# Projections as pairs of 64-column matmuls, and transposes as float32 matmuls with the identity, in a pipelined attention and ternary layer

## The chip, the cores and the metric

The kernel runs on one core of one Trainium2 chip. The metric is device time in microseconds (us). Of the kernel before, three runs took 470.35, 467.87 and 469.35 us; the median is 469.35.

## What is computed

The input x holds 32 sequences of 256 tokens with 128 features, in float32. Cut to what matters:

```python
def _L0_attn_ref(x, W_qkv, b_qkv, W_out, b_out):
    qkv = x @ W_qkv + b_qkv                    # 16 query heads, 4 key/value heads, 8 wide
    q, k, v = jnp.split(qkv, [DIM, DIM + KV_DIM], axis=-1)
    ...
    scores = jnp.einsum('bkgsd,bktd->bkgst', q, k) / np.sqrt(HEAD_DIM)
    scores = jnp.where(causal, scores, -jnp.inf)
    attn = jax.nn.softmax(scores, axis=-1)
    y = jnp.einsum('bkgst,bktd->bkgsd', attn, v)
    ...
    return y @ W_out + b_out

def _L0_ffn_ref(input, weight, alpha, bias):
    delta = 0.7 * jnp.mean(jnp.abs(weight))
    w = jnp.where(weight > delta, 1.0, jnp.where(weight < -delta, -1.0, 0.0)) * alpha
    return jnp.einsum('bsd,od->bso', input, w) + bias

x = x + _layernorm(_L0_attn_ref(_layernorm(x), ...))
x = x + _layernorm(_L0_ffn_ref(_layernorm(x), ...))
```

## The kernel before

All of x stays on chip in one tile X. The work on the 32 sequences is a pipeline written out by hand: in step t each engine runs its part of a fixed list once, and each function works on sequence t minus a lag of its own. The lags are NORM 0, PROJ 1, SPLIT 2, MAX 3, TURN 4, ATT 5, DIV 6, OUT 7, MID 8, FFN 9, and the store comes last, so there are 42 steps. There is no loop on the device and no scheduler: the order in which each engine meets its work is the order of the calls in its own `step`, and semaphores between engines do the rest. Each engine works strictly in that order, so a wait holds back all that stands behind it.

TensorE's `step` (L939 to L968) mixes short groups of matmuls. Scores (`st`, L813) and the products for the row maxima (`mx`, L862) are bf16 matmuls that fill 64 columns of the array each; they come in pairs, one for output partitions 0 to 63 and one for 64 to 127. The value projection (`v`, L877) does the same in float32. Attention times values (`pv`, L834) uses four 32-column matmuls, float32. Between them stand the groups that the change touches, all with 128 columns: `op` (L890, output projection, from tile yn), `x1` (L910, transposes of the normed input xn1), `ff` (L918, the ternary layer), `qk` (L927 and L928, query and key projection) and `x3` (L936, transposes of xn3). `turn` (L900) transposes the 16-row maxima. Two transposes of 128x128 are in `x1` and two in `x3`. All these groups, and `v`, write one shared PSUM bank, `ps_w`; `take` (L789) makes each wait until the user before it in ORDER = v, op, turn, x1, ff, qk, x3 has been read out.

The readers, with their places in their engines' orders:
- ScalarE: `take_y` (L477, copy of ps_y), exp 0 (L455), `second_part` (L491, bf16 split), exp 1, `take_turned` (L498), exp 2, `take_xn1` (L506), exp 3, exp 4, two norms of A (L468), `take_qk` (L513, L514), exp 5, `first_part` (L484), `take_xn3` (L522), two norms of F (L468).
- VectorE: two groups of row maxima (L651), `take_v` (L699), statistics (L609), `split_max` (L725 and L727: a cast of the maxima to bf16 and its remainder), moments (L621), `take_a` (L708, which frees ps_w from `op`), then more maxima, a reciprocal (L735), statistics, `take_f` (L716) and the norms (L628).
- GpSimd (POOL): `third` (L415, third part of the split), the inverse roots (L392 to L399), an addition (L407), `remainder` (L430), `divide` (L423, which writes yn), another addition (L407).
- SyncE (SP) issues every DMA of the steady steps in one queue; among them are the denominators (L328), their reciprocals to DRAM and back, spread over the partitions (rden, L343), and every fourth step a load and a store of 512 KB each.

In `pe.transpose` and `pe.matmul` alike the profile lists one or two TensorE records for each call: one for a transpose and for a bf16 matmul, two for a float32 matmul.

Of the kernel before, what the change touches and what calls it, by code (L numbers as in the profile page):

```python
# [11 lines left out]
B, S, D = 32, 256, 128  # L12
NH, NKV, HD = 16, 4, 8
G = NH // NKV
NLO = 2
# [17 lines left out]
NORM, PROJ, SPLIT, MAX, TURN, ATT, DIV, OUT, MID, FFN = range(10)  # L33
# [52 lines left out]
def build(nc, x, wq, wk, wv, wo, bq, bk, bo, wf, alpha, bf, ident, qfix, kfix, vmask, bvw, out):  # L86
    with ExitStack() as ctx:
        def sb(name, shape, dt):
            return ctx.enter_context(nc.sbuf_tensor(name, shape, dt))

        def psum(name, shape):
            return ctx.enter_context(nc.psum_tensor(name, shape, F32))

        def sem(name):
            return ctx.enter_context(nc.semaphore(name))


        wq_sb = sb("wq_sb", [D, 128], F32)
        wk_sb = sb("wk_sb", [D, 128], F32)
        wv_sb = sb("wv_sb", [D, 32], F32)  # L100
        wo_sb = sb("wo_sb", [128, NLO, D], F32)
# [7 lines left out]
        id_sb = sb("id_sb", [128, 128], F32)  # L109
# [12 lines left out]
        weff = sb("weff", [D, D], F32)  # L122
# [3 lines left out]
        xn1 = [sb(f"xn1_{i}", [128, TT, D], F32) for i in range(2)]  # L126
        xn1T = sb("xn1T", [128, S], F32)
# [20 lines left out]
        xn3 = [sb(f"xn3_{i}", [128, TT, D], F32) for i in range(2)]  # L148
        xn3T = sb("xn3T", [128, S], F32)
# [15 lines left out]
        ps_w = psum("ps_w", [128, 512])  # L165
# [22 lines left out]
        s_qk_ps = sem("s_qk_ps")  # L188
# [589 lines left out]
        def _(pe):  # L778
# [10 lines left out]
            def take(s, user):  # L789

                sm, v = last_work(s, user)
                if sm is not None:
                    pe.wait_ge(sm, v)
# [88 lines left out]
            def op(s):  # L882
                if s.on(OUT):
                    y = yn[s.b(OUT) % 2]

                    pe.wait_ge(s_yn, s.n(OUT, 1, 1))
                    take(s, "op")
                    for j in range(TT):
                        for lo in range(NLO):
                            last = pe.matmul(ps_w[:, D * j:D * j + D], y[:, lo, 128 * j:128 * j + 128],  # L890
                                             wo_sb[:, lo, :], start=(lo == 0), stop=(lo == NLO - 1))
                    last.then_inc(s_op_ps, 1)

            def turn(s):
# [9 lines left out]
            def x1(s):  # L904
                if s.on(PROJ):

                    pe.wait_ge(s_xn1, s.n(PROJ, 1, 1))
                    take(s, "x1")
                    for j in range(TT):
                        last = pe.transpose(ps_w[:, 128 * j:128 * j + 128], xn1[s.b(PROJ) % 2][:, j, :], id_sb[:])  # L910
                    last.then_inc(s_xt_ps, 1)

            def ff(s):
                if s.on(FFN):
                    pe.wait_ge(s_x3, s.n(FFN, 1, 1))
                    take(s, "ff")
                    for j in range(TT):
                        last = pe.matmul(ps_w[:, D * j:D * j + D], xn3T[:, 128 * j:128 * j + 128], weff[:],  # L918
                                         start=True, stop=True)
                    last.then_inc(s_ff_ps, 1)  # L920

            def qk(s):
                if s.on(PROJ):

                    pe.wait_ge(s_xt, s.n(PROJ, 1, 1))
                    take(s, "qk")
                    pe.matmul(ps_w[:, 0:S], wq_sb[:], xn1T[:], start=True, stop=True)  # L927
                    pe.matmul(ps_w[:, S:2 * S], wk_sb[:], xn1T[:], start=True, stop=True).then_inc(s_qk_ps, 1)  # L928

            def x3(s):  # L930
                if s.on(MID):

                    pe.wait_ge(s_xn3, s.n(MID, 1, 1))
                    take(s, "x3")
                    for j in range(TT):
                        last = pe.transpose(ps_w[:, 128 * j:128 * j + 128], xn3[s.b(MID) % 2][:, j, :], id_sb[:])  # L936
                    last.then_inc(s_x3_ps, 1)

            def step(s):  # L939
                st(s, 0)  # L940
                mx(s, 0)
                v(s)
                mx(s, 1)
                st(s, 1)
                mx(s, 2)
                op(s)
                st(s, 2)
                mx(s, 3)
                pv(s, 0)
                turn(s)  # L950
                st(s, 3)
                mx(s, 4)
                x1(s)
                pv(s, 1)
                pv(s, 2)
                ff(s)
                st(s, 4)
                mx(s, 5)
                qk(s)
                pv(s, 3)  # L960
                mx(s, 6)
                st(s, 5)
                mx(s, 7)
                pv(s, 4)
                x3(s)
                mx(s, 8)
                pv(s, 5)
                mx(s, 9)  # L968
# [63 lines left out]
```

## Time and profile before

| what | value |
|---|---|
| median of three runs | 469.35 us |
| the profiled execution | 467.76 us, span 465.9 us |
| TensorE matmuls (PE) | 413.6 us busy, 89% of the span, 6918 records |
| weight loads (PEld) | 287.2 us, 62% |
| VectorE (DVE) | 396.6 us, 85% |
| ScalarE (ACT) | 323.5 us, 69% |
| GpSimd (POOL) | 297.1 us, 64% |
| granted TensorE clock, mean | 0.965 of full |

Read it so: the busy share is over the whole span, with a filling stretch ahead of 89 us and an emptying one behind 404 us; in between, a step of the pipeline repeats. In a timeline each row is a group of like instructions in order of time: its start, how long from the first start to the last end, engine, line, operation, output and inputs, and the count. Matmuls overlap, so a group's end lies behind the start of the next; how long a group holds the engine is the distance from its start to the next group's start. The page's PEclk row shows 9 tenths or more of full speed in its 40 slices of 11.6 us, except for one slice at 8 (from 35 us) and the last three, at 7, 5 and 5 (from 431 us on).

### The profile page before, as it was taken

What the parts mean: (1) busy time and instruction counts of PE and PEld (TensorE: products, weight loads), DVE (VectorE), ACT (ScalarE), POOL (GpSimd) and SP (SyncE); (2) the same over time, 40 slices, a digit from 0 to 9 for tenths busy, and PEclk for the clock granted to TensorE, in tenths of its full rate; (3) what the DMA queues carried; (4) which work ended last, traced back from release to release, by engine and by line L of the source; (5) the groups of instructions that cost most, each with busy time, mean ns of one, the idle gap of its engine ahead of it and who ended that gap; (6) DMA issues with size and microseconds to landing.
All of it is one profiled execution on the core that took longest, in us unless ns stands there. A gap on an engine that the chain in (4) does not pass through costs nothing.

```text
span 465.9 us, 18300 instructions
## 1 busy us (share of the span) xinstructions
PE 413.6 (89%) x6918; PEld 287.2 (62%) x6918; DVE 396.6 (85%) x1307; ACT 323.5 (69%) x577; POOL 297.1 (64%) x552
## 2 busy tenths in 40 slices
PE   1478989999999999999999999999999999998541
PEld 1345657676776667676667677766777766664331
DVE  5768888999999899999999999989999998983441
ACT  1323877777787778788777777777888887767521
POOL 2523335567777677777777677767777776566663
PEclk9998999999999999999999999999999999999755
DMA  6454433354333633363334433363334333501211
GB/s 185 52 51 67 103 85 75 82 108 82 79 74 71 153 75 78 75 159 80 77 77 119 117 74 70 76 158 74 79 79 123 75 74 76 113 28 30 54 41 45
DMA packets 72255, 39.50 MB, mean 85 GB/s; under 512 B 13000, under 2 KB 68008, under 8 KB 72168
## 3 DMA queue, kind: packets, MB, share of 16 engines
q1 hardware_dynamic: 70832, 37.70, 36.8%
q8 instruction: 55, 0.90, 0.9%
q10 hardware_dynamic: 1336, 0.64, 0.5%
q14 instruction: 32, 0.26, 0.3%
HBM read 13.65 MB, written 4.72 MB: 39 GB/s over the span
## 4 chain that ended last, share of the span: by engine, by line
PE 58%; DVE 14%; DMA 8%; issue 7%; POOL 7%; ACT 2%; SPq 2%; ACTq 2%; POOLq 0%; DVEq 0%
PE ps_y L834 13%; PE ps_mx L862 11%; PE ps_st L813 11%; DVE M L651 7%; DMA den<-Y 5%; PE ps_w L890 5%; PE ps_w L927 4%; PE ps_w L918 4%; PE ps_w L928 3%; DVE stats L609 2%; POOL yn L423 2%; PE ps_w L936 2%; PE ps_w L910 2%; PE ps_w L900 2%; DVE Mp L725 1%
## 5 line engine op out<-in xcount | busy, mean ns | idle before, releaser
L651 DVE TENSOR_REDUCE M<-ps_mx 128x2 f32<-128x512 f32 (+3 forms) x448 | 218.6, 529 | 19.6 <-PE ps_mx L862 18.2
L455 ACT ACTIVATE PT<-ps_st 128x1024 f32<-128x1024 f32 (+1 forms) x192 | 168.6, 881 | 23.6 <-PE ps_st L813 12.5
L862 PE MATMUL ps_mx<-KS,QS 112*64 112x64 bf16 (+2 forms) x2560 | 130.6, 225 | 10.7 <-DMA KS<-part 6.4
L862 PEld LDWEIGHTS ps_mx<-KS,QS 112*64 112x64 bf16 x2560 | 88.2, 111 | 55.8 <-issue 26.6
L834 PE MATMUL ps_y<-PT,VB 128*32 128x256 f32 (+3 forms) x2048 | 103.0, 307 | 0.9 <-ACT PT L455 0.9
L813 PE MATMUL ps_st<-QS,KS 114*64 114x256 bf16 (+1 forms) x1024 | 103.7, 304 | 0.0
L395 POOL TENSOR_TENSOR rstd<-vareps,mhalf 128x2 f32<-128x2 f32 x128 | 88.8, 694 | 10.0
L430 POOL TENSOR_TENSOR rest<-QK,part 128x512 f32<-128x512 f32 x32 | 39.3, 1227 | 40.1 <-ACT part L484 40.1
L498 ACT CAST MpT<-ps_w 16x512 bf16<-16x512 f32 x32 | 18.4, 575 | 55.1 <-PE ps_w L900 55.1
L834 PEld LDWEIGHTS ps_y<-PT,VB 128*32 128x32 f32 x2048 | 40.3, 108 | 24.4 <-ACT PT L455 14.6
L813 PEld LDWEIGHTS ps_st<-QS,KS 114*64 114x64 bf16 x1024 | 47.1, 109 | 12.8 <-issue 2.2
L392 POOL TENSOR_TENSOR nmean<-mv,minus 128x2 f32<-128x2 f32 x64 | 12.6, 197 | 59.3 <-DVE mv L621 58.6
L423 POOL TENSOR_TENSOR yn<-Y,rden 128x512 f32<-128x512 f32 x32 | 40.9, 1277 | 9.2 <-DMA rden<-rec_dram 8.7
L890 PE MATMUL ps_w<-wo_sb,yn 128*128 128x128 f32 x256 | 38.4, 295 | 8.3 <-POOL yn L423 8.2
L393 POOL TENSOR_TENSOR vareps<-mv,eps 128x2 f32<-128x2 f32 x128 | 25.7, 201 | 30.8 <-DVE mv L621 30.8
L415 POOL TENSOR_TENSOR part<-rest,part 128x512 bf16<-128x512 f32 x32 | 37.2, 1163 | 6.1 <-ACT part L491 5.5
L628 DVE TENSOR_SCALAR xn<-X,mv,rstd 128x128 f32<-128x128 f32 x128 | 36.7, 344 | 5.1 <-POOL rstd L395 4.8
L890 PEld LDWEIGHTS ps_w<-wo_sb,yn 128*128 128x128 f32 x256 | 32.1, 197 | 11.3 <-POOL yn L423 10.1
L609 DVE BATCH_NORM_STATS2 stats<-X 128x6 f32<-128x128 f32 x128 | 29.0, 268 | 9.7 <-POOL X L407 7.2
L468 ACT ACTIVATE A<-A,shift,rstd 128x128 f32<-128x128 f32 x64 | 27.8, 483 | 12.1 <-POOL shift L399 12.0
L468 ACT ACTIVATE F<-F,shift,rstd 128x128 f32<-128x128 f32 x64 | 28.1, 487 | 3.3 <-POOL shift L399 3.3
L621 DVE BATCH_NORM_AGGREGATE mv<-stats 128x2 f32<-128x6 f32 x256 | 28.4, 160 | 1.9 <-issue 0.2
(62 smaller groups left out, 512.8 us busy)
## 6 DMA issues: line engine op xcount, KB each, us to landing
QS<-part SPq DMA_DIRECT2D x192, 64.0 KB
rden<-rec_dram SPq DMA_DIRECT2D x32, 256.0 KB
out<-X SPq DMA_DIRECT2D x8, 512.0 KB, 5.1
X<-in_x SPq DMA_DIRECT2D x7, 512.0 KB, 7.6
KS<-part SPq DMA_DIRECT2D x32, 96.0 KB
KS<-part SPq DMA_DIRECT2D x32, 64.0 KB
KS<-part SPq DMA_DIRECT2D x32, 32.0 KB
QS<-MpT SPq DMA_DIRECT2D x32, 16.0 KB
```

The lines of the kernel that those rows point to most:

```text
L395: gp.tensor_tensor(rstd[k][:], vareps[k][:], mhalf[:], ALU.pow).then_inc(s_rstd[k], 1)
L415: gp.tensor_tensor(part3[i][:], rest[:], part2[i][:], ALU.subtract).then_inc(s_p3, 1)
L423: gp.tensor_tensor(yn[i][:], Y[i][:], rden[i][:], ALU.mult).then_inc(s_yn, 1)
L430: gp.tensor_tensor(rest[:], QK[:], part1[s.b(PROJ) % RING][:], ALU.subtract).then_inc(s_r1, 1)
L455: nc.scalar.activation(PT[n % 2][:, 0:512 * banks], ps_st[n % 2][:, 0:banks, :].rearrange("p a c -> p (a c)"), ACT.Exp, scale=SCALE).then_ ...
L468: last = nc.scalar.activation(dst[i][:, j, :], src[i][:, j, :], ACT.Identity, bias=shift[k][:, j:j + 1], scale=rstd[k][:, j:j + 1])
L609: last = nc.vector.bn_stats(stats[k][:, j, :], src(j))
L651: last = nc.vector.tensor_reduce(m[:, pair:pair + pairs, i], ps_mx[n % 2][:, at:at + w].rearrange("p (h t) -> p h t", h=pairs), AX_X, ALU.max)
L813: last = pe.matmul(dst[64 * hi:64 * hi + 64, SLOT * slot:SLOT * (slot + nj)], k[:, 2 * hi + lo, key_block(i, diag), :], q[:, j:j + nj, h:h ...
L834: last = pe.matmul(ps_y[32 * g:32 * g + 32, lo, BL * i:S], v[:, at:at + 2, :].rearrange("p a c -> p (a c)"), p[:, g, slot:slot + NB - i, : ...
L862: last = pe.matmul(ps_mx[n % 2][64 * one:64 * one + 64, at:at + w], q[:, h, BL * i:BL * i + BL], k[:, kv, blocks, :], start=True, stop=Tru ...
L890: last = pe.matmul(ps_w[:, D * j:D * j + D], y[:, lo, 128 * j:128 * j + 128], wo_sb[:, lo, :], start=(lo == 0), stop=(lo == NLO - 1))
```

## The change

The five 128-column groups are issued as pairs of 64-column matmuls, one for each half of the output partitions. The four transposes of a step become such pairs too, of ordinary float32 matmuls with the identity as the moving operand. The order of the groups, the tiles, the waits and all other engines' work are as before.

```diff
 def op(s):
     ...
     for lo in range(NLO):
-        last = pe.matmul(ps_w[:, D * j:D * j + D], y[:, lo, 128 * j:128 * j + 128],
-                         wo_sb[:, lo, :], start=(lo == 0), stop=(lo == NLO - 1))
+        for h in (0, 64):
+            last = pe.matmul(ps_w[h:h + 64, D * j:D * j + D],
+                             y[:, lo, 128 * j + h:128 * j + h + 64], wo_sb[:, lo, :],
+                             start=(lo == 0), stop=(lo == NLO - 1), skip_group_check=True)
 def x1(s):
     ...
-        last = pe.transpose(ps_w[:, 128 * j:128 * j + 128], xn1[s.b(PROJ) % 2][:, j, :], id_sb[:])
+        for h in (0, 64):
+            last = pe.matmul(ps_w[h:h + 64, 128 * j:128 * j + 128],
+                             xn1[s.b(PROJ) % 2][:, j, h:h + 64], id_sb[:], start=True, stop=True,
+                             skip_group_check=True)
 def ff(s):
     ...
-        last = pe.matmul(ps_w[:, D * j:D * j + D], xn3T[:, 128 * j:128 * j + 128], weff[:],
-                         start=True, stop=True)
+        for h in (0, 64):
+            last = pe.matmul(ps_w[h:h + 64, D * j:D * j + D], xn3T[:, 128 * j + h:128 * j + h + 64],
+                             weff[:], start=True, stop=True, skip_group_check=True)
 def qk(s):
     ...
-    pe.matmul(ps_w[:, 0:S], wq_sb[:], xn1T[:], start=True, stop=True)
-    pe.matmul(ps_w[:, S:2 * S], wk_sb[:], xn1T[:], start=True, stop=True).then_inc(s_qk_ps, 1)
+    for at, w in ((0, wq_sb), (S, wk_sb)):
+        for h in (0, 64):
+            last = pe.matmul(ps_w[h:h + 64, at:at + S], w[:, h:h + 64], xn1T[:], start=True,
+                             stop=True, skip_group_check=True)
+    last.then_inc(s_qk_ps, 1)
 def x3(s):
     ...
-        last = pe.transpose(ps_w[:, 128 * j:128 * j + 128], xn3[s.b(MID) % 2][:, j, :], id_sb[:])
+        for h in (0, 64):
+            last = pe.matmul(ps_w[h:h + 64, 128 * j:128 * j + 128],
+                             xn3[s.b(MID) % 2][:, j, h:h + 64], id_sb[:], start=True, stop=True,
+                             skip_group_check=True)
```

## Rows read from the trace of the kernel before

**Rows 1.** Busy time by stretch: us, PE, PEld, DVE, ACT, POOL (records), clock, DMA share, GB/s

```profile
89.12:403.62 314.50, 308.60 (x5399) 217.35 (x5395) 295.88 (x989) 248.19 (x445) 226.27 (x420) 1.00 0.40 91
241.53:253.86 12.33, 12.33 (x221) 8.75 (x217) 11.79 (x41) 9.95 (x19) 9.19 (x17) 1.00 0.34 79
253.86:267.30 13.44, 12.63 (x220) 8.65 (x216) 11.90 (x41) 10.17 (x19) 9.18 (x17) 1.00 0.54 143
```

**Rows 2.** Timeline of TensorE in one step: start, length, line, tiles, shapes, count

```profile
243.29 0.39 PE L862 MATMUL ps_mx<-KS,QS 112*64 112x256 bf16 x4
243.51 0.60 PE L877 MATMUL ps_w<-wv_sb,xn1T 128*64 128x32 f32 x16
...
244.61 0.40 PE L862 MATMUL ps_mx<-KS,QS 112*64 112x64 bf16 x12
244.94 1.16 PE L890 MATMUL ps_w<-wo_sb,yn 128*128 128x128 f32 x8
246.03 0.41 PE L813 MATMUL ps_st<-QS,KS 114*64 114x256 bf16 x4
...
246.60 0.64 PE L834 MATMUL ps_y<-PT,VB 128*32 128x256 f32 x8
247.16 0.38 PE L900 MATMUL ps_w<-idb,Mp 128*16 128x128 bf16 x4
...
247.94 0.39 PE L862 MATMUL ps_mx<-KS,QS 112*64 112x128 bf16 x8
...
248.65 0.86 PE L834 MATMUL ps_y<-PT,VB 128*32 128x64 f32 x24
249.44 0.71 PE L918 MATMUL ps_w<-weff,xn3T 128*128 128x128 f32 x4
250.08 0.62 PE L813 MATMUL ps_st<-QS,KS 114*64 114x256 bf16 x6
250.54 0.39 PE L862 MATMUL ps_mx<-KS,QS 112*64 112x256 bf16 x4
250.86 0.70 PE L927 MATMUL ps_w<-xn1T,wq_sb 128*128 128x256 f32 x2
...
251.92 0.64 PE L834 MATMUL ps_y<-PT,VB 128*32 128x256 f32 x8
252.49 0.41 PE L862 MATMUL ps_mx<-KS,QS 112*64 112x256 bf16 x4
252.73 0.39 PE L813 MATMUL ps_st<-QS,KS 114*64 114x256 bf16 x4
...
253.86 0.44 PE L936 MATMUL ps_w<-id_sb,xn 128*128 128x128 f32 x2
```

**Rows 3.** Timeline of ScalarE, from its split to the copy of xn3T

```profile
241.32 0.61 ACT L484 CAST part<-QK 128x512 bf16<-128x512 f32 x1
242.00 0.37 ACT L522 COPY xn3T<-ps_w 128x256 f32<-128x256 f32 x1
...
244.43 0.62 ACT L491 CAST part<-rest 128x512 bf16<-128x512 f32 x1
```

**Rows 4.** Timeline of GpSimd in the same step

```profile
245.13 1.16 POOL L415 TENSOR_TENSOR part<-rest,part 128x512 bf16<-128x512 f32 x1
```

**Rows 5.** Timeline of VectorE in the same step

```profile
245.58 0.74 DVE L725 CAST Mp<-M 128x32 bf16<-128x32 f32 x1
...
246.63 0.39 DVE L708 TENSOR_TENSOR A<-ps_w,bo_sb 128x256 f32<-128x256 f32 x1
```

**Rows 6.** Timeline of TensorE at the same place of another step

```profile
95.02 0.64 PE L834 MATMUL ps_y<-PT,VB 128*32 128x256 f32 x8
95.47 0.39 PE L900 MATMUL ps_w<-idb,Mp 128*16 128x128 bf16 x4
```

**Rows 7.** Waits, 100 to 385 us: total us, times, longest

```profile
POOL yn L423 <- DMA rden<-rec_dram: 2.8, 7, 0.7
```

**Rows 8.** Line 890 from 400 us on: count, shortest, median and longest ns

```profile
L890 PE MATMUL ps_w<-wo_sb,yn x40: 275/275/581, 407.6 to 446.9; 128*128 128x128 f32 x40
```

## The prediction, made before the changed kernel was run

> **What bounds the kernel now.** I read the busy times by stretch first. From the first `x3` at 89.12 us to the 26th at 403.62 us TensorE is busy 308.60 of 314.50 us [rows 1], so 25 periods of 12.58 us each. The undisturbed period is 12.33 us with PE busy for all of it; one with the load and the store of 512 KB lasts 13.44 [rows 1]. That looks like a kernel bound by TensorE. A busy PE need not be one at work, though, so I next measured in the timeline how long each group holds the engine, from start to start.
>
> The place to look at is `turn`. Its group starts 0.56 us after the eight float32 matmuls of `pv` ahead of it [rows 2]. In another step the same neighbours are 0.45 us apart [rows 6], so TensorE stands still for 0.11 us here and no busy digit shows it. The timeline of VectorE tells for what: `take_a`, which frees ps_w for `turn`, ends at 246.63 + 0.39 = 247.02, and `turn` is seen at 247.16 [rows 2, 5]. From there I followed the releases backwards. `take_a` stands behind the cast of the maxima, which lasts 0.74 us for 32 elements and ends at 246.32, 0.03 us after POOL's L415 ends at 246.29 [rows 4, 5]. L415 starts at 245.13, 0.08 after ScalarE's L491 ends at 245.05 [rows 3, 4]. ScalarE works on without a gap from the copy of xn3T at 242.00, and this copy comes 0.03 us behind the end of `x3`: the next `x3` starts at 253.86 and ends 0.44 later, at 254.30, and one period back that is 241.97 [rows 2, 3]. So the period is a loop of two pieces: from the end of `x3` over ScalarE, POOL and VectorE to `turn`, 247.16 - 241.97 = 5.19 us, and from `turn` to the end of `x3` on TensorE, 254.30 - 247.16 = 7.14 us. Together 12.33. Of the five changed groups `op` lies in the first piece, beside the loop; `x1`, `ff`, `qk` and `x3` lie in the second, on it.
>
> **Prices.** Four bf16 matmuls of 256 columns in 64-column pairs hold the engine 0.22 us (243.29 to 243.51), 0.11 a pair [rows 2]. Eight float32 ones of 256 columns, four side by side, hold it 0.45 [rows 6], so 0.22 for one starting time: float32 streams at half the rate, and 128 float32 columns should take 0.11. Sixteen float32 matmuls of `v` take 0.60 us in all, overlapped ends included [rows 2], so float32 pairs do run side by side in 64-column form. Hence 0.11 us for a float32 pair of 128 columns and 0.22 for one of 256. Going from one width to another costs more: 256-column `mx` before `qk` holds 0.32 us, before `v` only 0.22 [rows 2]; a switch costs 0.10. The first pair behind a switch costs 0.02 more (252.49 to 252.73 is 0.24, against 0.22) [rows 2]. For a float32 pair I take that 0.02 as well; it could be nothing, or 0.06, half of the weights of a 128-column load.
>
> **Part by part**, each call being two records, so each call of two halves is two pair times:
> - `ff`: held 0.64 (249.44 to 250.08), now 4 x 0.11 + 0.02 = 0.46, and `st` behind it loses its 0.02: -0.20 [rows 2].
> - `qk` with the `mx` ahead: held 1.38 (250.54 to 251.92), now 0.22 + 4 x 0.22 + 0.10 = 1.20: -0.18 [rows 2].
> - `x1` with the `mx` ahead: held 0.71 (247.94 to 248.65), now 4 x 0.055 (bf16 pairs of 128 columns) + 4 x 0.11 + 0.10 = 0.76: +0.05 [rows 2].
> - `x3`: its end counts. Group length 0.44 now, later 0.02 + 3 x 0.11 + 0.275 (one record, [rows 8]) = 0.625: +0.185 [rows 2].
> - `op` with the `mx` ahead: held 1.42 (244.61 to 246.03), now (0.33 - 0.10) + 8 x 0.11 = 1.11, and 0.02 behind: -0.33 [rows 2]. I cost this gain at nothing: `take_a` ends when the loop lets it. The 0.11 us of standing before `turn` should grow to about 0.5.
>
> On the loop: -0.20 - 0.18 + 0.05 + 0.185 = -0.145 us, a period of 12.19. What is late next? ScalarE's own route: L484 ends at 241.93 and the copy of xn3T starts at 242.00, so that route has 0.07 of room [rows 3], and L484 itself moves 0.15 earlier with `st` 4 behind `ff`. Together 0.22, more than 0.145.
>
> Not every period can give it. The mean is 0.25 us over the undisturbed one [rows 1], with about half of the 25 disturbed by DMA: POOL waits for rden [rows 7], or VectorE for the denominators behind the 512 KB. A DMA that is late is late in absolute time, so I count these at half: 12.5 x 0.145 + 12.5 x 0.07 = 2.7 us. While the pipeline fills, without `ff` and `x3`, I take 4 periods of -0.13 = 0.5. While it empties, at half clock in the end (records of 581 ns for 275, [rows 8]), `op` and `ff` are on the path of the last eight periods: by the first weights and the switches some 0.15 each period, 1.2, less 0.4 for the last `x3`, whose two transposes become four pairs at half clock. Sum: 2.7 + 0.5 + 0.8 = 4.0 us. The profiled execution, 467.76 us, should come to 463.8; it lies 1.6 under the median, so the median goes from 469.35 to 465.3.
>
> The Trainium skill (TensorEngine Tiling (Array Packing), Key Properties) says that changing the tiling mode, not just the tile, drains TensorE. The 0.10 us between widths agrees with it [rows 2]; six such drains fewer per step would by that rule alone be 0.6 us per step, some 15 us in all. That is the first rival's size, and the trace speaks against it.
>
> **Rivals.**
> - *TensorE's own work decides*, and the 0.11 us at `turn` is no loop but chance. Then every group counts: -0.33 - 0.20 - 0.18 + 0.05, and for `x3`, held 0.46 for 0.37, +0.07 with the `mx` behind: -0.59 us, 25 times 14.8, with 1.3 at the ends: 453.3 us. For it stands PE's 12.33 of 12.33; against it the three releases 0.03 to 0.08 us apart. Chance 0.06.
> - *DMA takes the gain.* The loop shortens, but rden has almost no room [rows 7] and the load and store recur every fourth period [rows 1], so the later periods wait for what the earlier ones saved. Only the ends gain: 468.0 us. Chance 0.22.
> - *Weights of a float32 pair are not hidden behind the pair before.* `v` takes 0.60 us for eight pairs of only 32 columns, the last one's length of some 0.2 included, so about 0.055 a pair, where 32 columns would stream in 0.03: that is loading [rows 2]. If this adds to the 0.11 rather than lying beside it, the sixteen pairs of `x1`, `ff`, `qk` and `x3` cost 0.88 us more per period: -0.145 + 0.88 = +0.735, and 469.35 + 25 x 0.735 = 487.7 us; at a third of it 473. It turns slower from 0.01 us per pair on. Against it: bf16 pairs hide their load fully. The transposes are where it would bite first, since one record becomes four. That pairs do not run side by side at all (0.11 more per pair) is the same case at its worst, and would mean the change does not do what it says; the sixteen matmuls of `v` in 0.60 us nearly exclude it. Chance 0.12.
>
> **How the numbers follow.** The loop forecast has 0.60, with its own range 462 to 467.5. An interval of 0.5% is 2.35 us, about what a measurement can tell from no change: faster means under 467.0. Of the forecast's 0.60, 0.55 lies below that; with the first rival that makes 0.62. Same: 0.05, 0.21 of the DMA case and 0.02 of a weak weight case, 0.28. Slower: 0.10. The range leaves out the first rival below and most of the third above: 460.0 to 470.5.
>
> **What would show it.** Right: undisturbed periods of about 12.19 us from `x3` to `x3`; `op` held about 0.9 us instead of 1.09; an idle time of PE before `turn`, released by VectorE's A, of 0.4 to 0.5 us a step; the cast still ending with POOL's L415. `ff` at 0.46, `qk` at 0.98 instead of 1.06, pairs 0.11 apart. Wrong: a period near 11.75 with no idle time at `turn` (first rival); undisturbed periods shorter but the mean still 12.58 (second); pairs of 128 columns 0.12 us or more apart, or TensorE's part from `turn` to the end of `x3` over 7.14 us (third).

## The result, and the profile after

The change made the kernel 1.2% slower: 475.66 us (median of 20 runs, 470.81 to 479.86) against 470.18 us (20 runs, 464.64 to 474.24) for the kernel before. The ratio is 1.012, with a 95% interval from 1.009 to 1.015. Medians and ranges are of all runs of a kernel, while the ratios leave out the runs that took over 1.5% more than its fastest. The forecast was 465.3 us, faster; the measured time lies outside its range too. The profiled execution took 476.13 us.

The same stretches as in [rows 1], for the changed kernel: first from the first `x3` to the 25th, then two undisturbed periods. Columns: stretch, us, busy us (records) of PE, PEld, DVE, ACT and POOL, granted clock, DMA share, GB/s.

```profile
91.58:397.81 306.23, 295.49 (x5861) 215.28 (x5857) 286.34 (x955) 239.07 (x432) 218.78 (x405) 1.00 0.40 91
244.02:256.63 12.61, 12.26 (x248) 8.96 (x244) 11.91 (x41) 9.94 (x19) 9.17 (x17) 1.00 0.38 84
269.94:282.56 12.62, 12.27 (x249) 8.96 (x245) 11.91 (x41) 9.94 (x19) 9.21 (x17) 1.00 0.35 78
```

An undisturbed period went from 12.33 to 12.62 us, where 12.19 was forecast. TensorE is busy for less of it than before, 12.26 against 12.33 us, and the period is still longer: busy time of TensorE does not set it.

The timeline of TensorE for that period answers to [rows 2].

```profile
244.02 0.66 PE L946 MATMUL ps_w<-id_sb,xn 128*64 128x128 f32 x8
...
245.20 0.41 PE L862 MATMUL ps_mx<-KS,QS 112*64 112x128 bf16 x8
245.45 0.60 PE L813 MATMUL ps_st<-QS,KS 114*64 114x256 bf16 x6
...
247.20 0.41 PE L862 MATMUL ps_mx<-KS,QS 112*64 112x64 bf16 x12
247.44 1.07 PE L891 MATMUL ps_w<-wo_sb,yn 128*64 128x128 f32 x16
248.34 0.39 PE L813 MATMUL ps_st<-QS,KS 114*64 114x256 bf16 x4
...
248.90 0.64 PE L834 MATMUL ps_y<-PT,VB 128*32 128x256 f32 x8
249.89 0.38 PE L902 MATMUL ps_w<-idb,Mp 128*16 128x128 bf16 x4 [0.35 <-DVE A L708]
...
250.66 0.39 PE L862 MATMUL ps_mx<-KS,QS 112*64 112x128 bf16 x8
251.03 0.66 PE L913 MATMUL ps_w<-id_sb,xn 128*64 128x128 f32 x8
251.61 0.86 PE L834 MATMUL ps_y<-PT,VB 128*32 128x64 f32 x24
252.41 0.66 PE L924 MATMUL ps_w<-weff,xn3T 128*64 128x128 f32 x8
252.89 0.61 PE L813 MATMUL ps_st<-QS,KS 114*64 114x256 bf16 x6
253.33 0.39 PE L862 MATMUL ps_mx<-KS,QS 112*64 112x256 bf16 x4
253.68 0.65 PE L935 MATMUL ps_w<-xn1T,wq_sb 128*64 128x256 f32 x4
...
254.69 0.64 PE L834 MATMUL ps_y<-PT,VB 128*32 128x256 f32 x8
```

Read it from start to start. `op` holds TensorE 0.90 us instead of 1.09, and the `mx` ahead of it 0.24 instead of 0.33: the width switch is gone and the pairs run side by side, 0.11 us each. `ff` holds it 0.48 instead of 0.64, `qk` 1.01 instead of 1.06. All that `op` saved is then spent in front of `turn`: `pv` and `turn` are 0.99 us apart, against 0.45 where nothing is waited for [rows 6], so TensorE stands 0.54 us where it stood 0.11 (the part of the 0.43 that `op` did not save comes from the later end of `x3`, where the loop starts). It waits for `take_a`, which is still behind the cast, and the cast still ends with POOL's L415:

```profile
247.85 1.16 POOL L415 TENSOR_TENSOR part<-rest,part 128x512 bf16<-128x512 f32 x1 [0.27 <-ACT part L491]
```

```profile
248.18 0.87 DVE L725 CAST Mp<-M 128x32 bf16<-128x32 f32 x1
...
249.35 0.39 DVE L708 TENSOR_TENSOR A<-ps_w,bo_sb 128x256 f32<-128x256 f32 x1
```

`x1` holds TensorE 0.58 us instead of 0.35, and the `mx` ahead of it is not a bit shorter, 0.37. That last number is the one that I had not foreseen. A group of the same shape, also followed by a 64-column group but with nothing to wait for, holds it 0.25 us in the same period (245.20 to 245.45): some 0.12 us of the 0.37 are a wait. What for is in the timelines of ScalarE, VectorE and the weight loads:

```profile
244.72 0.37 ACT L522 COPY xn3T<-ps_w 128x256 f32<-128x256 f32 x1 [0.30 <-PE ps_w L946]
...
250.31 0.57 ACT L498 CAST MpT<-ps_w 16x512 bf16<-16x512 f32 x1 [1.60 <-PE ps_w L902]
```

```profile
253.11 0.42 DVE L716 TENSOR_TENSOR F<-ps_w,bf_sb 128x256 f32<-128x256 f32 x1 [0.20 <-PE ps_w L924]
```

```profile
250.99 0.45 PEld L913 LDWEIGHTS ps_w<-id_sb,xn 128*64 128x64 f32 x8
...
253.65 0.23 PEld L935 LDWEIGHTS ps_w<-xn1T,wq_sb 128*64 128x64 f32 x4 [0.20 <-issue]
```

ScalarE's read of `turn`'s result ends at 250.31 + 0.57 = 250.88, and the first weights of `x1` load at 250.99, 0.11 us later. VectorE's read of `ff` ends at 253.53 and the first weights of `qk` load at 253.65, 0.12 later. At `turn` it is 249.74 to 249.85, 0.11 again. The shared bank ps_w passes from reader to TensorE at these two places as it does at `turn`. The three distances are 0.11 to 0.12 us in each of the first 24 periods of the changed kernel. In the kernel before, the same two rows of ScalarE and of the weight loads were:

```profile
247.58 0.57 ACT L498 CAST MpT<-ps_w 16x512 bf16<-16x512 f32 x1 [1.61 <-PE ps_w L900]
```

```profile
248.27 0.20 PEld L910 LDWEIGHTS ps_w<-id_sb,xn 128*128 128x128 f32 x2
```

248.15 to 248.27 is 0.12 us again, and it is 0.11 in all 24 periods. `x1` was released by the read of `turn` before the change too, and no view marks it as a wait: the release came at about the time when TensorE was through with the switch of width, since the `mx` ahead, held 0.36, would by itself have taken 0.25 and 0.10. At `qk` it was different. There the distance was 0.24 us in most periods before the change, so nothing was waited for and some 0.12 us were free.

### The profile page after: what moved, and what is told of

The parts are those of the page before. It is cut to its first block, busy times and chain, and to the rows that moved or that the text cites. A ratio compares the mean times of both kernels' runs of the same rounds, so it can differ in the third digit from the quotient of the medians.

```text
span 474.3 us, 20092 instructions
## 1 busy us (share of the span) xinstructions
PE 414.4 (87%) x7814; PEld 296.4 (62%) x7814; DVE 397.6 (84%) x1307; ACT 322.7 (68%) x577; POOL 297.0 (63%) x552
## 4 chain that ended last, share of the span: by engine, by line
PE 51%; DVE 22%; issue 9%; DMA 6%; POOL 4%; ACT 3%; SPq 2%; ACTq 2%; POOLq 0%; DVEq 0%
PE ps_y L834 12%; DVE M L651 11%; PE ps_mx L862 8%; PE ps_st L813 8%; PE ps_w L935 7%; PE ps_w L924 4%; PE ps_w L946 4%; PE ps_w L913 4%; DVE Mp L725 3%; DMA den<-Y 3%; DVE stats L609 3%; DMA KS<-part 2%; PE ps_w L891 2%; PE ps_w L902 2%; POOL yn L423 2%
## 5 line engine op out<-in xcount | busy, mean ns | idle before, releaser
L862 PEld LDWEIGHTS ps_mx<-KS,QS 112*64 112x64 bf16 x2560 | 91.6, 111 | 49.3 <-DVE M L651 17.7
L813 PEld LDWEIGHTS ps_st<-QS,KS 114*64 114x64 bf16 x1024 | 52.3, 110 | 7.7 <-issue 4.0
L891 PE MATMUL ps_w<-wo_sb,yn 128*64 128x128 f32 x512 | 37.2, 291 | 9.2 <-POOL yn L423 9.1
L415 POOL TENSOR_TENSOR part<-rest,part 128x512 bf16<-128x512 f32 x32 | 37.2, 1162 | 10.8 <-ACT part L491 10.4
L891 PEld LDWEIGHTS ps_w<-wo_sb,yn 128*64 128x64 f32 x512 | 29.7, 145 | 11.1 <-POOL yn L423 11.0
L468 ACT ACTIVATE A<-A,shift,rstd 128x128 f32<-128x128 f32 x64 | 27.8, 484 | 11.7 <-POOL shift L399 11.7
```

The costliest lines, as they stand in the source:

```text
L415: gp.tensor_tensor(part3[i][:], rest[:], part2[i][:], ALU.subtract).then_inc(s_p3, 1)
L468: last = nc.scalar.activation(dst[i][:, j, :], src[i][:, j, :], ACT.Identity, bias=shift[k][:, j:j + 1], scale=rstd[k][:, j:j + 1])
L813: last = pe.matmul(dst[64 * hi:64 * hi + 64, SLOT * slot:SLOT * (slot + nj)], k[:, 2 * hi + lo, key_block(i, diag), :], q[:, j:j + nj, h:h ...
L862: last = pe.matmul(ps_mx[n % 2][64 * one:64 * one + 64, at:at + w], q[:, h, BL * i:BL * i + BL], k[:, kv, blocks, :], start=True, stop=Tru ...
L891: last = pe.matmul(ps_w[h:h + 64, D * j:D * j + D], y[:, lo, 128 * j + h:128 * j + h + 64], wo_sb[:, lo, :], start=(lo == 0), stop=(lo == ...
```

## The experiments

Three theories were put against each other. Each ratio below is to the kernel before as it was run beside the others (medians 468.33 to 468.99 us). Theory 1: the period is a loop over the readers of ps_w. From the end of `x3` it runs over ScalarE, POOL and VectorE to `turn`, then over ScalarE's read into MpT to `x1`, `pv`, `ff`, `take_f`, `qk`, `pv` and `x3`. Theory 2: the time for which the groups hold TensorE sets it. Theory 3: pairs cost something that the timeline does not show.

### Parts of the change alone

The changed kernel with the transposes as before, in `x1` and, with xn3 for xn1, in `x3` (`op`, `ff`, `qk` stay pairs); the diff is against the changed kernel:

```diff
-for h in (0, 64):
-    last = pe.matmul(ps_w[h:h + 64, 128 * j:128 * j + 128], xn1[s.b(PROJ) % 2][:, j, h:h + 64],
-                     id_sb[:], start=True, stop=True, skip_group_check=True)
+last = pe.transpose(ps_w[:, 128 * j:128 * j + 128], xn1[s.b(PROJ) % 2][:, j, :], id_sb[:])
```

> The changed kernel with the four transposes put back as they were: op, ff and qk stay pairs. Theory 1, the loop: the undisturbed period runs from the end of x3 over ScalarE, POOL and VectorE to turn, and on TensorE from turn over the readers of ps_w (MpT before x1, take_f before qk) to the end of x3. op lies beside it. take_f is held by VectorE's own order, so qk can start only 0.13 us earlier; its own length gives 0.05. Period 12.33 - 0.18 = 12.16 us, time about 1% under before, 465 to 467. Theory 2, TensorE's own holding time sets the period: op -0.28, ff -0.15, qk -0.15 and more, a period of 11.7, some 15 us faster. Theory 3, pairs cost something everywhere that the timeline does not show: slower than before even without the transposes.

464.81 us (12 runs); ratio to before 0.9915 (0.9878 to 0.9951). An undisturbed period is 12.13 us, and TensorE is busy for 11.91 of it.

Only the transposes changed, in `x1` and likewise in `x3`, with `op`, `ff` and `qk` as in the kernel before:

```diff
-last = pe.transpose(ps_w[:, 128 * j:128 * j + 128], xn1[s.b(PROJ) % 2][:, j, :], id_sb[:])
+for h in (0, 64):
+    last = pe.matmul(ps_w[h:h + 64, 128 * j:128 * j + 128], xn1[s.b(PROJ) % 2][:, j, h:h + 64],
+                     id_sb[:], start=True, stop=True, skip_group_check=True)
```

> Only the transposes are changed to pairs of float32 matmuls. Theory 1, the loop: x1 cannot start before MpT is read, so its whole added length, 0.25 us, falls on the loop, and x3 adds 0.22 plus 0.01: period 12.33 + 0.48 = 12.81 us, worse than the whole change (12.62), some 2 to 2.5% slower than before, about 480 us. Theory 2, holding time: x1 +0.25, x3 +0.12, period 12.70, no larger than that. Forecast as made before the result (x1 +0.05, x3 +0.185): 12.57.

476.82 us (4 runs); ratio 1.016 (1.011 to 1.022). The undisturbed period is 12.81 us, as theory 1 says to the hundredth; the total rose less than the 2 to 2.5% expected, and the last section of experiments gives a likely reason.

Only `op`, and only `x3`, each against the kernel before:

```diff
-last = pe.matmul(ps_w[:, D * j:D * j + D], y[:, lo, 128 * j:128 * j + 128],
-                 wo_sb[:, lo, :], start=(lo == 0), stop=(lo == NLO - 1))
+for h in (0, 64):
+    last = pe.matmul(ps_w[h:h + 64, D * j:D * j + D], y[:, lo, 128 * j + h:128 * j + h + 64],
+                     wo_sb[:, lo, :], start=(lo == 0), stop=(lo == NLO - 1), skip_group_check=True)
```

```diff
-last = pe.transpose(ps_w[:, 128 * j:128 * j + 128], xn3[s.b(MID) % 2][:, j, :], id_sb[:])
+for h in (0, 64):
+    last = pe.matmul(ps_w[h:h + 64, 128 * j:128 * j + 128], xn3[s.b(MID) % 2][:, j, h:h + 64],
+                     id_sb[:], start=True, stop=True, skip_group_check=True)
```

> Only op is changed to pairs. Theory 1: period stays 12.33 us, the time within 0.3% of before; TensorE stands before turn for some 0.4 us in place of 0.1, waiting for VectorE's A. Theory 2: period 12.05, 7 us faster.

> Only x3 is changed to pairs of float32 matmuls. Theory 1: its end comes 0.22 us later and the copy of xn3T another 0.01: period 12.56 us, about 1% slower, 474 to 476. Theory 2: x3 holds TensorE 0.12 longer: period 12.45. If ScalarE's own route to the copy of xn3T bounded, nothing: 12.33.

Only `op`: 468.16 us (12 runs), ratio 0.9997 (0.9968 to 1.0026), no change. Only `x3`: 472.64 us (8 runs), ratio 1.008 (1.005 to 1.012). One undisturbed period of each of the four, in the order above (t1, t2, t3, t4):

```profile
102.04:114.17 12.13, 11.91 (x236) 8.44 (x232) 11.72 (x41) 9.94 (x19) 9.18 (x17) 1.00 0.49 120
```

```profile
197.06:209.87 12.81, 12.76 (x232) 9.27 (x228) 11.94 (x41) 9.96 (x19) 9.18 (x17) 1.00 0.33 78
```

```profile
190.39:202.72 12.33, 12.11 (x229) 8.61 (x225) 11.79 (x41) 9.96 (x19) 9.18 (x17) 1.00 0.40 85
```

```profile
192.27:204.84 12.57, 12.52 (x227) 9.03 (x223) 11.93 (x41) 9.96 (x19) 9.21 (x17) 1.00 0.40 85
```

12.13, 12.81, 12.33 and 12.57, where theory 1 had 12.16, 12.81, 12.33 and 12.56, and theory 2 had 11.7, 12.70, 12.05 and 12.45. The parts add up: -0.20 for `op`, `ff` and `qk` and +0.48 for the transposes make +0.28, and the whole change has +0.29. Of the transposes' 0.48, `x3` alone is 0.24 and so `x1` 0.24. Theory 3 falls with t1, which is faster than before. In t3, 0.22 us of TensorE's busy time went from the undisturbed period (12.11 for 12.33) and the period stayed: that is theory 2's end.

### Moving the release of ps_w

If the loop runs over `take_a`, the place of `take_a` in VectorE's order must matter. One edit in VectorE's `step`, tried on four kernels:

```diff
 def step(s):
     ...
+    take_a(s)
     split_max(s)
     moments(s, MID, 2)
-    take_a(s)
```

> The kernel before, with one edit on VectorE: take_a is called ahead of split_max, so that ps_w is freed before the cast that waits for POOL, and turn waits for Mp alone. Theory 1: the release of turn moves up 0.47 us, but TensorE has only 0.1 us of standing time there: period 12.33 to 12.23 us, at most 0.5% faster. Theory 2 (TensorE's holding time alone): nothing, 12.33.

> The same edit on VectorE with only op as pairs, which alone had left the period at 12.33. Theory 1: the 0.28 us that op saves can now reach turn: period 12.33 - 0.38 = 11.95, 1 to 2% faster than before. If op's gain was lost for another reason than take_a's place behind the cast, 12.23 as with the kernel before.

> The same edit on VectorE with the whole change. Theory 1: TensorE stands 0.53 us before turn there, so all 0.47 us of the earlier release count: period 12.62 to 12.15 us, the time under that of the kernel before, 466 or less. Theory 2: 12.62 stays.

> The same edit on VectorE with op, ff and qk as pairs and the transposes as before. Theory 1: period 12.14 - 0.38 = 11.76 us undisturbed; DMA disturbs more periods, since a shorter period leaves rden less room, so the mean gains less: 456 to 461 us, 2 to 2.5% faster than before. Theory 2: as without the edit, 12.14.

| kernel, with `take_a` first | undisturbed period: expected, measured | time us | ratio to before |
|---|---|---|---|
| kernel before | 12.23, 12.23 | 467.46 (10 runs) | 0.997 (0.994 to 1.001) |
| only `op` as pairs | 11.95, 11.95 | 465.22 (12) | 0.993 (0.990 to 0.996) |
| the whole change | 12.15, 12.10 | 467.12 (10) | 0.992 (0.988 to 0.997) |
| `op`, `ff`, `qk` as pairs | 11.76, 11.91 | 464.10 (7) | 0.991 (0.987 to 0.994) |

The first ratio is not clear of 1. The third is the least certain: it rests on six of the ten runs, and by the medians of all runs (467.12 against 468.33 us) it would be 0.997. Read the third row against the first, too: with `take_a` first, the whole change shortens the undisturbed period by 0.13 us, but the intervals of the two ratios overlap. The profile of the third row is of an execution that took 472.36 us, so only its undisturbed period is used.

The second line, an undisturbed period of the kernel with only `op` changed, and under it the longest period of the same run:

```profile
219.36:231.31 11.95, 11.95 (x229) 8.51 (x225) 11.23 (x41) 9.95 (x19) 9.18 (x17) 1.00 0.32 79
153.51:169.31 15.80, 13.85 (x228) 9.10 (x224) 12.14 (x42) 10.69 (x19) 9.30 (x18) 0.89 0.55 137
```

This is the cleanest proof of the loop: the same pairs in `op` are worth nothing behind the cast (12.33 to 12.33) and 0.28 us an undisturbed period with `take_a` ahead of it (12.23 to 11.95). VectorE is busy 11.23 us there instead of 11.79, since the cast now comes when POOL's L415 is nearly done:

```profile
222.96 1.16 POOL L415 TENSOR_TENSOR part<-rest,part 128x512 bf16<-128x512 f32 x1
```

```profile
223.80 0.42 DVE L708 TENSOR_TENSOR A<-ps_w,bo_sb 128x256 f32<-128x256 f32 x1 [0.30 <-PE ps_w L891]
224.14 0.17 DVE L725 CAST Mp<-M 128x32 bf16<-128x32 f32 x1
```

L415 ends at 224.12, and the cast lasts 0.17 us instead of 0.74. In the kernel before the cast ended 0.03 to 0.04 us after L415 in 21 of the 24 periods; in the other three it had started just ahead of L415 and took 0.16 to 0.28 us. The Trainium skill (SBUF — State Buffer, Who interferes with whom) says that casts on VectorE can use a pair of ports that VectorE shares with GpSimd, and that of two such operations the second is fully blocked until the first is through; the cast's end 0.03 us after POOL's L415 [rows 4, 5] agrees.

The times gained less than the periods: 465.2, 0.7% less than before, where 1 to 2% were expected, 467.1 for 466 or less, 464.1 for 456 to 461. The long periods got longer, up to 15.80 us here. From 100 to 385 us, VectorE's wait for the denominators grew from the first of these rows, of the kernel before, to the second, of the kernel with `op` as pairs and `take_a` first (total us, times, longest). POOL's wait for rden grew more, from 2.8 us in 7 waits [rows 7] to the third row:

```profile
DVE rec L735 <- DMA den<-Y: 4.5, 4, 1.4
```

```profile
DVE rec L735 <- DMA den<-Y: 5.3, 5, 2.1
```

```profile
POOL yn L423 <- DMA rden<-rec_dram: 5.7, 14, 0.8
```

The miss in the periods is the fourth line, 11.91 for 11.76. With `turn` free, the next hand-over of ps_w is late. In that kernel the `mx` group ahead of `qk` holds TensorE 0.50 us, against 0.35 in the changed kernel. Its timelines of TensorE, VectorE and the weight loads:

```profile
246.81 0.60 PE L813 MATMUL ps_st<-QS,KS 114*64 114x256 bf16 x6
247.24 0.39 PE L862 MATMUL ps_mx<-KS,QS 112*64 112x256 bf16 x4
247.74 0.65 PE L932 MATMUL ps_w<-xn1T,wq_sb 128*64 128x256 f32 x4
```

```profile
245.94 1.32 DVE L651 TENSOR_REDUCE M<-ps_mx 128x2 f32<-128x384 f32 x3
247.18 0.41 DVE L716 TENSOR_TENSOR F<-ps_w,bf_sb 128x256 f32<-128x256 f32 x1
```

```profile
247.71 0.23 PEld L932 LDWEIGHTS ps_w<-xn1T,wq_sb 128*64 128x64 f32 x4 [0.34 <-issue]
```

`take_f` follows VectorE's row maxima without a gap, its read ends at 247.59, and the weights of `qk` load 0.12 us later; 0.15 us is just what is missing.

### What the large transfers hide

The undisturbed period grew by 0.29 us, but the first 24 periods together by only 2.8 us in the two profiles (306.23 against 303.43 us, both from the first `x3`). That is 0.12 each. The two kernels were run with the 512 KB transfers taken out of the steady part:

```diff
 def load_x(s):
-    if s.t0 % GRP == 2 and s.t0 < B - GRP:
-        g = s.group(2 - GRP)
+    if 2 <= s.t0 <= B // GRP:
+        g = s.t0 - 1
     ...
 def store_x(s):
-    if s.on(STORE) and s.b(STORE) % GRP == GRP - 1:
+    if s.b(STORE) == B - 1:
         ...
+        for g in range(B // GRP):
+            sp.dma_start(ov[bass.ds(g, 1)].rearrange("n p r d -> (n p) r d"), rows(g)).then_inc(s_store, 16)
```

> The kernel before, with the 512 KB loads of x issued one per step from step 2 to step 8 and all stores at the end, so that no such transfer runs in the steady part; the computation is the same. If these transfers are what lengthens some periods, all periods between the 8th and the 24th are 12.33 us with a spread under 0.1. If it is the smaller transfers of the split parts and of rden, the lengthened ones stay. The total time may go either way by the stores at the end, some 20 us, and is not the point.

> The same for the changed kernel: all periods between the 8th and the 24th at 12.62 us. Then the whole price of the change, 0.29 us, falls on every period, and this kernel is slower than the one without the change by 24 x 0.29 = 7 us in that part, against 24 x 0.12 = 2.8 us measured with the transfers in place. If the DMA does not cushion the change, the difference stays at 0.12.

Before, then changed, from the first `x3` to the 25th, each with its longest period:

```profile
94.31:393.03 298.72, 296.89 (x5188) 209.90 (x5185) 284.57 (x955) 238.36 (x432) 218.17 (x405) 1.00 0.34 76
380.31:393.03 12.72, 12.41 (x220) 8.74 (x217) 11.44 (x35) 9.95 (x19) 8.27 (x15) 1.00 0.33 80
```

```profile
94.15:398.64 304.49, 294.85 (x5861) 215.53 (x5857) 286.19 (x955) 238.15 (x432) 218.26 (x405) 1.00 0.33 75
347.81:360.77 12.96, 12.45 (x248) 9.04 (x245) 12.24 (x41) 9.94 (x19) 9.16 (x17) 1.00 0.33 76
```

304.49 - 298.72 = 5.8 us, 0.24 a period instead of 0.12, and the totals are 482.55 us before and 487.73 us changed (2 runs each). The expectation was half right. The periods of 13.4 us and more are gone, so they come from the 512 KB transfers; but periods up to 0.4 us over the undisturbed one remain, so the smaller transfers lengthen some by themselves. In the period of 12.72 us that ends at 206.81 in the kernel before so altered, it is POOL's wait for rden:

```profile
196.17 1.27 POOL L422 TENSOR_TENSOR yn<-Y,rden 128x512 f32<-128x512 f32 x1 [0.44 <-DMA rden<-rec_dram]
```

The 512 KB transfers cost the 24 periods of the kernel before 4.7 us (303.43 - 298.72) and those of the changed kernel 1.7 (306.23 - 304.49): the shorter loop loses more to them, by one execution of each. That t2 rose by less than its period would follow from the same, but t2 was not run without the transfers.

Last, loads and stores of 256 KB every second step in place of 512 KB every fourth. This was done to the kernel before, and to the one of the table's last row (`op`, `ff` and `qk` as pairs, the transposes as before, `take_a` first):

```diff
-GRP = 4
+GRP = 2
 def load_x(s):
-    if s.t0 % GRP == 2 and s.t0 < B - GRP:
-        g = s.group(2 - GRP)
+    if (s.t0 + 2) % GRP == 0 and s.t0 < B - 2:
+        g = s.group(-2)
```

> The kernel before with loads and stores of 256 KB in every second step in place of 512 KB in every fourth. If queueing behind one large transfer is what lengthens a period, no period lasts over 13.0 us in the steady part, but twice as many are touched; the mean of 12.64 falls to about 12.45 and the time by 1%, to 463 to 466. If the bytes alone count, the mean stays.

> op, ff and qk as pairs, transposes as before, take_a ahead of split_max, and transfers of 256 KB. Undisturbed period 11.91 as without the last edit; if large transfers cause the lengthened periods, which are up to 14.3 us there, the mean falls from 12.41 to about 12.1 and the time from 464 to 456 to 460, 2 to 2.5% under before. If bytes alone count: 464 as without.

On the kernel before: 467.05 us (10 runs), ratio 0.995 (0.992 to 0.999), less than the 1% expected; the first 24 periods take 300.28 us instead of 303.43 and one still lasts 13.07. The expectation that no period would last over 13.0 us failed, narrowly. On the last row's kernel: 459.14 us (6 runs), ratio 0.981 (0.976 to 0.986), the fastest kernel of this study. The time is within the 456 to 460 us expected, but the mean of its 24 periods fell from 12.41 to 12.28 us only, where 12.1 was expected:

```profile
89.96:384.58 294.62, 287.53 (x5572) 201.32 (x5568) 270.23 (x955) 241.00 (x432) 218.57 (x405) 1.00 0.41 96
188.69:200.59 11.90, 11.80 (x236) 8.35 (x232) 11.19 (x41) 10.05 (x19) 9.16 (x17) 1.00 0.40 85
```

## Why the prediction was wrong

- **The loop** was right, and with it that `op` is worth nothing. The end of `x3` (244.02 + 0.66 = 244.68) to `turn` (249.89) takes 5.21 us, against 5.19 before. The standing time before `turn` was forecast at about 0.5 and is 0.54. What failed is the second piece, from `turn` to the end of `x3`: it was to shrink and took 7.40 us, against 7.14.
- **The prices of a pair** were right: 0.11 us for 128 float32 columns, and 0.10 for a width switch; the `mx` ahead of `op` lost 0.09. The rule of the Trainium skill (TensorEngine Tiling (Array Packing), Key Properties) that a change of mode drains TensorE agrees with that 0.09; what the switches saved came back as waiting at `turn`, `x1` and `qk`. The rival in which weights of a float32 pair are not hidden named the right sign and the wrong cause: of its two signs, the part from `turn` to the end of `x3` over 7.14 us came, but the pairs stayed 0.11 us apart.
- **`x1`, +0.05, failed most.** The step let the `mx` ahead shrink from 0.36 to its streams, "now 4 x 0.055 (bf16 pairs of 128 columns) + 4 x 0.11 + 0.10", as if all above them were drain. `x1` was released by the read into MpT there, and a switch that falls away inside a wait gives nothing. Measured +0.24: the group itself grew by 0.23 (0.35 to 0.58), and the `mx`, which was to lose 0.14, took 0.37. That `x1` hangs on this read rests on the 0.11 us in every period and on the sums of t1 to t4; no run moved the read itself.
- **`ff` and `qk`, -0.20 and -0.18 as a sum on the loop, failed next.** `take_f` lies between them: `qk` starts 0.12 us after VectorE's read ends, and the rest of `ff`'s gain and that of the `mx` ahead of `qk` ended there. From start to start, `ff` and `st` took 0.92 us instead of 1.10, nearly as forecast, but the `mx` with `qk` 1.36 instead of 1.38, where 1.20 was forecast. Measured together by t1, where `op` counts nothing: -0.20 in place of -0.38.
- **`x3`, +0.185, was mis-sized**: t4 shows +0.24. The group lasts 0.66 us where 0.625 was forecast, since its first pair costs 0.04 more than the next rather than 0.02; the rest is how long the copy behind it lags.
- **"What is late next?"** was asked of ScalarE's route alone. It had to be asked of each of the seven users of ps_w.
- By sum, -0.145 should have been +0.24 - 0.20 + 0.24 = +0.28, and 24 or 25 such periods, half of them cushioned by DMA, are 3 to 7 us. The measured 5.5 lies within. How much of it belongs to the filling and the emptying part, which the forecast let gain 1.3 us, is open: of the 8.4 us between the two profiled executions only 2.8 lie in the first 24 periods, while without the 512 KB transfers 5.8 lie there, of 5.2 between the medians. The first `x3` starts at 89.12 us before and 91.58 after, but also at 88.40 in t3 and 92.25 in the second kernel with `take_a` first, so one execution tells nothing of 2 us there.

## What to carry to other kernels

Where several groups take turns in one PSUM bank, the loop runs through every read of that bank, and a saving on TensorE counts only up to the next read. Check each user before pricing an edit: the end of the reader ahead against the first weight load, not against the first matmul and not by the listed waits; a distance that is the same and this short in every period, here 0.11 us, points to a wait even where TensorE looks busy, while the 0.24 us at `qk` before the change was slack. And look for the release that could move: calling `take_a` earlier, ahead of a cast that stood behind another engine, took the kernel with the whole change from 1.2% over the kernel before to 0.8% under it by the ratio, or 0.3% by the medians. An undisturbed period of the kernel before gains 0.10 us by the same edit and one of the changed kernel 0.52. The kernels that gained most clearly keep the transposes as they were.

## What was unexpected of the hardware

A wait of 0.1 us leaves no mark in the busy time: TensorE was busy 12.33 of 12.33 us while it stood 0.11 us at `turn` and was released at `x1` by a read that had just ended. And a disturbed period can be paid a second time, by the clock. The 15.80 us period above has a mean granted clock of 0.89, while the period of 11.95 us stays at 1.00. Three stretches within it:

```profile
162.00:165.00 3.00, 1.05 (x11) 0.44 (x10) 2.97 (x15) 1.89 (x3) 1.54 (x6) 1.00 0.19 44
165.00:166.00 1.00, 1.00 (x8) 0.62 (x12) 0.97 (x5) 0.53 (x3) 0.88 (x3) 0.99 0.36 96
166.00:169.00 3.00, 3.00 (x44) 1.70 (x43) 2.39 (x8) 1.85 (x4) 1.60 (x3) 0.50 0.39 99
```

TensorE was busy 1.05 of 3 us, and 1 us later the granted clock stood at 0.50, the lower of the two levels, 1.2 GHz, for the 3 us shown. Not every such stretch does this: in the 14.30 us period of the kernel of the table's last row TensorE was busy 1.08 us from 111 to 113 us, and the clock stayed at 1.00.
